# Reordering the first units of a decoder-layer kernel: scores, transposed scores, maxima rows and input fetches

## The reference

```
x = layernorm(x + attn(x))            # 16 heads of 16, causal within a window of 64
x = layernorm(x + xattn(x, ctx))      # relu on q, k, v; causal; + q; its own layernorm
x = layernorm(x + ffn(x))             # 8 experts, top 2, two groups, capacity 160 each
```

## Time and profile before

| | us |
|---|---|
| median of 3 runs | 633.37 (625.5 to 636.76) |
| the profiled execution | 631.15 |
| its span | 629.4 |
| PE busy in the span | 524.6 (83%) |
| DVE, ACT, POOL busy | 337.2, 218.4, 147.0 |

### The profile page before, as it was taken

The page is one execution under the profiler, slowest core; times in us unless marked ns, Lnnn a source line. Parts: engine busy times, 40 slices in busy tenths (PEclk is TensorE's granted clock), DMA queues, the critical chain, the costliest instruction groups (busy, mean ns, idle before and its releaser), DMA issues. The chain is left out here.

```text
span 629.4 us, 12845 instructions
## 1 busy us (share of the span) xinstructions
PE 524.6 (83%) x5092; PEld 405.5 (64%) x5092; DVE 337.2 (54%) x952; ACT 218.4 (35%) x491; POOL 147.0 (23%) x160
## 2 busy tenths in 40 slices
PE   5067749889889999999999889699898999999960
PEld 4044527666667676666677656477677888888850
DVE  3436524665767877877768967774364112242114
ACT  2001223534435445544545525352521011222103
POOL 5010002101102102102223257000213755231330
PEclk9667788989989999999999989799999999999995
DMA  3999473492492591592556565455667634898214
GB/s 116 202 190 170 142 187 46 62 118 45 65 119 37 82 141 29 78 138 34 78 79 93 76 114 167 64 185 185 198 224 254 202 53 74 234 291 266 22 16 140
DMA packets 56760, 78.97 MB, mean 125 GB/s; under 512 B 9294, under 2 KB 49357, under 8 KB 53628
## 3 DMA queue, kind: packets, MB, share of 16 engines
q1 hardware_dynamic: 42524, 39.64, 38.5%
q10 hardware_dynamic: 8032, 33.21, 16.8%
q0 software_dynamic: 6144, 5.29, 5.2%
HBM read 40.32 MB, written 13.74 MB: 86 GB/s over the span
## 5 line engine op out<-in xcount | busy, mean ns | idle before, releaser
L938 DVE TENSOR_REDUCE negm<-nat 128x4 f32<-128x512 f32 (+2 forms) x192 | 120.1, 641 | 98.9 <-PE nat L521 97.1
L755 ACT ACTIVATE probs<-byk 128x512 f32<-128x512 f32 (+1 forms) x192 | 105.9, 563 | 114.0 <-PE byk L521 112.3
L521 PE MATMUL nat<-arena 96*128 96x128 bf16 (+2 forms) x512 | 73.8, 248 | 0.0
L521 PE MATMUL byk<-arena 99*128 99x128 bf16 (+2 forms) x512 | 71.6, 242 | 0.0
L1192 POOL TENSOR_TENSOR resk<-fk,parts_k 128x512 f32<-128x512 f32 x8 | 9.3, 1158 | 229.2 <-ACT fk L697 194.6
L517 PE MATMUL nat<-window_q,identb 128*128 128x384 bf16 (+1 forms) x96 | 36.0, 375 | 28.3 <-DMA arena<-parts_k 21.5
L521 PEld LDWEIGHTS nat<-arena 96*128 96x128 bf16 x512 | 47.0, 102 | 16.9 <-issue 3.5
L521 PEld LDWEIGHTS byk<-arena 99*128 99x128 bf16 x512 | 45.6, 99 | 17.4 <-issue 0.9
L517 PE MATMUL byk<-window_k,identb 128*128 128x384 bf16 (+1 forms) x96 | 34.0, 354 | 15.1 <-DMA arena<-mT 14.5
L659 PE MATMUL work<-yn_T,arena 128*128 128x160 f32 x256 | 40.1, 305 | 2.4 <-DVE r_s L1103 2.4
L659 PE MATMUL work<-woT,arena 128*128 128x160 f32 x256 | 39.8, 304 | 0.0
(11 more groups left out here) (189 smaller groups left out, 917.2 us busy)
## 6 DMA issues: line engine op xcount, KB each, us to landing
arena<-parts_q SPq DMA_DIRECT2D x96, 128.0 KB, 5.1
arena<-parts_k SPq DMA_DIRECT2D x96, 128.0 KB, 5.4
arena<-in_ffn_wi ACTq DMA_DIRECT2D x12, 1024.0 KB, 5.1
arena<-in_ffn_wo ACTq DMA_DIRECT2D x12, 1024.0 KB, 8.3
expert_x<-fq ACTq DMA_DIRECT2D x1, 2600.0 KB, 12.6
v_s<-expert_x SPq DMA_DIRECT2D x20, 130.0 KB
xres<-in_x ACTq DMA_DIRECT2D x1, 2048.0 KB, 28.1
token_y<-xres SPq DMA_DIRECT2D x8, 256.0 KB, 4.7
```

What stands on the lines that cost most here:

```text
L521: last = nc.tensor.matmul(bank[:, i * w:(i + 1) * w], lhsT, rhs, start=False, stop=(i == heads - 1), skip_group_check=True)
L755: nc.scalar.activation(dst, src, ACT.Exp, scale=0.25).then_inc(exp_ready, 1)
L938: V.tensor_reduce(dst, src, AX, ALU.max, negate=True).then_inc(nat_free[job % 2], 1)
```

## The change

- Unit 0's twelve N jobs run without a break. QS2, KS2 and VS0 move behind them and behind MP0 and MT0; T0.0 follows before N1.0. In PE's order: N0.0 to N0.11, MT0, QS2, KS2, VS0, T0.0, N1.0, T0.1, N1.1, and so on; QS3 comes after N1.5.
- T, PV, YA, YB, Y2, WO, R3 and L3 come sooner by 6.05, 4 and 2 slots in units 0, 1 and 2 (`SOONER`), MT at 11.5, 12.6 and 13.2 instead of 14. In unit 1 PE's order becomes N1.11, N2.0, MT1, N2.1, PV0.3, T1.0.
- In units 0 to 2 ACT issues the three DMAs of the maxima rows itself, right after its copy to mT, and SP doesn't.
- `LOADS` has new slots. x_T of batch 2, the value weights and `rows` go out only when unit 0's k stack has landed (a wait on ACT); x_T of batch 3 after KS2; woT, the cross attention's weights, the contexts and the router's weights at slots 16 to 50.
- xres is fetched batch by batch (XL, 256 KB each) at 8 slots into an s unit (14 in unit 0), each with a semaphore of its own.
- The clear of expert_x becomes four DMAs of 650 KB, in the s units of batches 4 to 7, from a pattern in `ranked`, with runs of 1040 bytes where there were 4160. The wait for it moves from ACT's QC to DVE's GA, before `ranked` is first written; POOL's GS keeps its own.
- The memset of the cross attention's value tile moves behind SK1 on DVE.

```diff
-LOADS = ((-20, 0), (-17.3, 1), (-16, 2), (-5, 3), (-4, 4), (2, 5), (6, 6), (14, 7), (22, 8), (26, 9))
+LOADS = ((-20, "x1"), (-16, "one_s"), (-4, "one_c"), (-3, "x2"), (-2.9, "wv"), (-2.8, "rows"), (11.84, "x3"), (16, "wo"), (20.5, "ck"), (21, "c0"),
+         (26, "cq"), (40, "c1"), (41, "cv"), (50, "wr"))
+CLEARS = (4, 5, 6, 7)
+SOONER = {0: 6.05, 1: 4, 2: 2}
+ROWS_BY_ACT = 3
...
-    return first_slot(k) + 18 + j
+    return first_slot(k) + 18 - SOONER.get(k, 0) + j
...
-                    add(n0 + 9.6, "LX", UNIT_OF["s", later])
+                    add(n0 + (14.6 if b == 0 else 9.6), "LX", UNIT_OF["s", later])
...
+            add(n0 + (14 if b == 0 else 8), "XL", k)
+            for at, name in ((-12.4, "QS"), (-12.35, "SQ"), (-12.3, "KS"), (-12.2, "SK")) if b == 2 else ((-19, "QS"), (-18, "SQ"), (-17.5, "KS"), (-16.5, "SK")):
+                add(n0 + at, name, k)
+            for at, name in ((11.85 if b == 0 else 8.5, "VS"), (20, "XB"), (34 - sooner, "Y2"), (35 - sooner, "WO"), (36 - sooner, "R3"), (36.8 - sooner, "L3")):
...
-        add(n0 + 12, "MP", k)
-        add(n0 + 14 if k < last else 195.6, "MT", k)
+        add(n0 + (11.3 if k == 0 else 12), "MP", k)
+        add(n0 + {0: 11.5, 1: 12.6, 2: 13.2}.get(k, 14) if k < last else 195.6, "MT", k)
...
             def MT(k, n, layer, b):
+                if k < ROWS_BY_ACT:
+                    return
                 emptied(sp, "MT", k)
...
                 nc.scalar.activation(mT[:, k % 2, :], bank[0:MR * H, :].bitcast(BF16)[:, 0:T], ACT.Copy).then_inc(released("MT", k), 1)
+                if k < ROWS_BY_ACT:
+                    emptied(act, "MT", k)
+                    for i in range(MR):
+                        nc.scalar.dma_start(stack["q", k % PAIRS][KR + i:KR + i + 1, :, :], mT[i * H:(i + 1) * H, k % 2, :])\
+                            .then_inc(m_rows[k % 2], 16)
...
+                if what in ("x1", "x2", "x3"):
+                    to = int(what[1])
+                    if to == 2:
+                        act.wait_ge(stacked["k"][0], SIDE)
+                    nc.scalar.dma_start(x_T(to), a["x_T"][to]).then_inc(x_in[to], 16)
...
+            def XL(k, n, layer, b):
+                nc.scalar.dma_start(xres[:, b * QT:(b + 1) * QT, 0:D], x_v[:, b * QT:(b + 1) * QT, :]).then_inc(xres_in[b], 16)
...
-                if b == 0:
-                    act.wait_ge(zeros_ready, 1)
-                    nc.scalar.dma_start(x_dram.rearrange("(p n a) d -> p n (a d)", p=P, a=4),
-                                        no_rows.unsqueeze(1).broadcast_to([P, E * GROUPS * CAP // P // 4, 4 * ROW])).then_inc(cleared, 16)
+                if b in CLEARS:
+                    part = E * GROUPS * CAP // P // len(CLEARS)
+                    at = CLEARS.index(b) * part
+                    if at == 0:
+                        act.wait_ge(zeros_ready, 1)
+                    nc.scalar.dma_start(x_dram.rearrange("(p n) d -> p n d", p=P)[:, at:at + part, :],
+                                        no_rows.unsqueeze(1).broadcast_to([P, part, ROW])).then_inc(cleared, 16)
```

More of the change, by code:

```diff
@@ L93, in in_order @@
         n0 = first_slot(k)
+        sooner = SOONER.get(k, 0)
         if layer == "s":
@@ L96, in in_order @@
                 if earlier == b:
-                    add(n0 + 9.6, "LX", UNIT_OF["s", later])
+                    add(n0 + (14.6 if b == 0 else 9.6), "LX", UNIT_OF["s", later])
             if b == 3:
                 add(n0 + 9.7, "LC", UNIT_OF["c", 2])
-            for at, name in ((-19, "QS"), (-18, "SQ"), (-17.5, "KS"), (-16.5, "SK"), (8.5, "VS"), (20, "XB"),
-                             (34, "Y2"), (35, "WO"), (36, "R3"), (36.8, "L3")):
+            add(n0 + (14 if b == 0 else 8), "XL", k)
+            for at, name in ((-12.4, "QS"), (-12.35, "SQ"), (-12.3, "KS"), (-12.2, "SK")) if b == 2 else ((-19, "QS"), (-18, "SQ"), (-17.5, "KS"), (-16.5, "SK")):
+                add(n0 + at, name, k)
+            for at, name in ((11.85 if b == 0 else 8.5, "VS"), (20, "XB"), (34 - sooner, "Y2"), (35 - sooner, "WO"), (36 - sooner, "R3"), (36.8 - sooner, "L3")):
                 add(n0 + at, name, k)
@@ L114, in in_order @@
             add(t_slot(k, j), "T", k, j)
-        add(n0 + 12, "MP", k)
-        add(n0 + 14 if k < last else 195.6, "MT", k)
+        add(n0 + (11.3 if k == 0 else 12), "MP", k)
+        add(n0 + {0: 11.5, 1: 12.6, 2: 13.2}.get(k, 14) if k < last else 195.6, "MT", k)
         for g in range(G):
[L118 to L121, removed]
+            add(n0 + 22.2 - sooner + 3 * g if k < last - 1 else t_slot(k, 3 * g + 2) + (1.1 if g < G - 1 else 0.5), "PV", k, g)
+        add(n0 + 32.6 - sooner if k < last - 1 else (198.6, 206.9)[k - last + 1], "YA", k)
+        add(n0 + 32.9 - sooner if k < last - 1 else (198.7, 207.0)[k - last + 1], "YB", k)
+    for i, (at, _) in enumerate(LOADS):
         add(at, "LD", i)
@@ L278, in flat @@
             return tile[tuple([slice(None)] * len(tile.shape))].rearrange(f"p {names} -> p ({names})")
-        no_rows = flat(fq, "s c t")[:, X1S * C * T - 4 * ROW:]
+        no_rows = flat(ranked, "a t e")[:, 0:ROW]
         wi, wo = [], []
@@ L300, in attention_and_experts @@
         ws_in = sem("ws_in"); bias_in = sem("bias_in"); w_s_v_in = sem("w_s_v_in"); rows_in = sem("rows_in"); w_s_o_in = sem("w_s_o_in")
-        wc_in = {n: sem(f"w_c_{n}_in") for n in "qkv"}; wr_in = sem("wr_in"); xres_in = sem("xres_in")
+        wc_in = {n: sem(f"w_c_{n}_in") for n in "qkv"}; wr_in = sem("wr_in"); xres_in = sems("xres_in", B)
         x_in = sems("x_in", TOK + 1); c_in = sems("c_in", TOK)
@@ L716, in QC @@
                     computed(act, "FQ", UNIT_OF["c", b - X1S])
-                elif b == 1:
-                    act.wait_ge(cleared, 16)
                 parts_free("q", k)
@@ L787, in LD @@
             def LD(i, n, layer, b):
[L789 to L792, removed]
+                what = LOADS[i][1]
+                if what in ("x1", "x2", "x3"):
[3 more added lines that the diff above has]
+                    nc.scalar.dma_start(x_T(to), a["x_T"][to]).then_inc(x_in[to], 16)
+                elif what in ("c0", "c1"):
+                    to = int(what[1])
+                    nc.scalar.dma_start(cT[:, to, :, :], a["ctx_T"][to]).then_inc(c_in[to], 16)
+                elif what in ("cq", "ck", "cv"):
+                    nc.scalar.dma_start(wc[what[1]][:, :, :], a["w_" + "_".join(what)]).then_inc(wc_in[what[1]], 16)
+                elif what == "wv":
@@ L793, in LD @@
                     nc.scalar.dma_start(ws[:, :, 2 * D:3 * D], a["w_s_v"]).then_inc(w_s_v_in, 16)
-                elif i == 2:
+                elif what == "rows":
                     nc.scalar.dma_start(rows[:, :, :], a["rows"].partition_broadcast(P)).then_inc(rows_in, 16)
[L796 to L799, removed]
+                elif what == "wo":
@@ L800, in LD @@
                     nc.scalar.dma_start(woT[:, :, :], a["w_s_o"]).then_inc(w_s_o_in, 16)
[L801 to L810, removed]
+                elif what == "wr":
@@ L811, in LD @@
                     nc.scalar.dma_start(wr[:, :, :], a["w_router"]).then_inc(wr_in, 16)
+            x_v = a["x"].rearrange("b (t p) d -> p (b t) d", p=P)
+            def XL(k, n, layer, b):
+                nc.scalar.dma_start(xres[:, b * QT:(b + 1) * QT, 0:D], x_v[:, b * QT:(b + 1) * QT, :]).then_inc(xres_in[b], 16)
             def WL(i, n, layer, b):
@@ L858, in _ @@
             walk({"QS": QS, "KS": KS, "KC": KC, "QC": QC, "XC": copy_out("XC", x1_T), "Y2": copy_out("Y2", yn_T, "WO"),
-                  "XR": copy_out("XR", x2_T, "RT"), "MT": MT, "T": T_, "PV": PV, "R1": R1, "R2": R2, "R3": R3, "GC": GC, "XB": clear, "LD": LD, "WL": WL,
+                  "XR": copy_out("XR", x2_T, "RT"), "MT": MT, "T": T_, "PV": PV, "R1": R1, "R2": R2, "R3": R3, "GC": GC, "XB": clear, "XL": XL, "LD": LD, "WL": WL,
                   "XT": XT, "H0": hidden("H0", range(0, 3)), "H2": hidden("H2", range(6, 8)), "FR": FR, "FN": FN})
@@ L898, in LD @@
             def LD(i, n, layer, b):
-                if i in (2, 3):
-                    link(V.memset(vone["sc"[i - 2]][:, :, :, :, :], 1.0))
+                if LOADS[i][1] in ("one_s", "one_c"):
+                    link(V.memset(vone[LOADS[i][1][4]][:, :, :, :, :], 1.0))
             def SC(k, n, layer, b):
@@ L1042, in GA @@
                 emptied(dve, "RT", UNIT_OF["c", (n + 1) * GB - 1])
+                if n == 0:
+                    dve.wait_ge(cleared, 16 * len(CLEARS))
                 tiles = slice(n * GT, (n + 1) * GT)
@@ L1196, in XB @@
             def XB(k, n, layer, b):
-                if b == 0:
-                    pool.wait_ge(xres_in, 16)
+                pool.wait_ge(xres_in[b], 16)
                 if b == 0:
@@ L1224, in GS @@
                         pool.wait_ge(numbered, 1)
-                        pool.wait_ge(cleared, 16)
+                        pool.wait_ge(cleared, 16 * len(CLEARS))
                     put_gates(tile, GT, 0)
```

## The result

The kernel after the change takes 625.12 us (median; 622.7 to 632.02), the kernel before beside it 633.05: a ratio of 0.9894, with a 95% interval of 0.9877 to 0.9912. It is 1.1% faster, where 611 us, 3.2% under the profiled execution before, were forecast, and 625 lies above the range. The profiled execution took 624.59 us (span 622.8), 6.6 us under the one before.

The account below looks back on a forecast made before the run. It took a start waiting for DMA, then a long run bound by PE. Lead to T0.0 17.9, plus T1.0 3.3, less T2.0 1, made 20.2 us: 631.15 to 611 us, forecast 603 to 618 (chance 0.75), range 600 to 623.

Parts of the forecast that it names:

- Step 1: Unit 0's k stack lands earlier without bulk loads: N0.0 at 26.0 instead of 36.3 us, gain 10.3 (0 to 12.8).
- Step 2: From N0.0 to T0.0: T0.0 at 45.1 us (43 to 47) instead of 66.58; lead including unit 0's stack 17.9.
- Step 3: PE's waits at MT1 and T1.0 for unit 1's maxima: 5.8 us instead of 9.1, gain 3.3 (0.3 to 4.7).
- Step 4: T2.0 charged 1 us (0 to 5.4); clear and residual in parts, moved memset and moved waits cost 0.
- The postponed loads collide one stage later: At QS3, N2.0 and T1.0: transfers land as in the crowded start, 10.5 us more, 621.5 us; chance 0.14.
- The stack copies set their own pace: At N0.0: 12 copies land no sooner without bulk loads, N0.0 near 36, 10.3 us lost, 621 us; chance 0.07.
- ScalarE is held: Among T0's and T1's exps: issuing six 256 KB loads holds ACT, at 8.97 us each 665 us; chance 0.04.

## Why the prediction was wrong

The direction held: faster, the gain won in the start and carried to the end whole, and no sign of the long run being bound by anything but PE. The size, 20.2 us, did not hold. Step by step:

**Step 1, unit 0's stack.** Forecast 26.0, measured 28.5 us. The step took the landing of six copies with the queue otherwise empty. Here twelve follow each other at 118 GB/s: by that rate 12 x 128 KB from 14.0 us on are done at 27.3 (an estimate). A loss of 2.5 us. The mechanism was right: with the old fetching N0.0 is at 36.8.

**Step 2, T0.0.** Forecast 45.1, measured 49.4: the 2.5 above and 1.8 more. MT0 came nearly as worked out (11.35 us behind N0.0 for 11.0); x_T 2 cost 1.1 us, as it had to wait for unit 1's copies; and QS2 and KS2 ran at the low clock, where the middle of both had been taken (granted 0.53 from 40 to 44 us):

```profile
41.27 6.56 PE L478 MATMUL work<-xT,ws 128*128 128x256 f32 x16 [1.13 <-DMA xT<-in_x_T]
```

QS3 found its input, so the 1.5 us charged there were not spent.

**Step 3, T1.0: the step that failed.** I took a landing of 3.3 us for unit 1's rows, "nearer to the quiet landing, because ACT's and SP's large transfers are spaced out by then". They were not: unit 3's twelve copies end their issue in the very moment in which the rows start theirs, and the rows land when these copies are through, 9 us after the last issue. PE's two waits were 11.7 us (1.2 at MT1) instead of 5.8: 5.9 us lost. Holding the copies back leaves 2.6 us at T1.0, so they are what the step left out. My upper bound, 6.3 us, was no bound: it was the median landing of one busy stretch of the old order, not worked out from the copies that would stand ahead in the new one. The old trace already went beyond it: T0.0 at 66.58 came 7.5 us after the issue of its rows ended at 59.1, and unit 2's copies had been issued just ahead of these rows, too:

```profile
52.05 3.84 SPq L390 DMA_DIRECT2D arena<-parts_k  x6
```

And part of what PE wins before T1.0 becomes a longer wait there: with the early loads MT1 came 3.8 us sooner than after the change (64.8 us instead of 68.6) and T1.0 only 2.3.

**Step 4, the rest.** T2.0 was charged 1 us; it cost 2.2 and another 1.3 at QC of the first cross unit. For that the timelines of ScalarE and PE have the reason:

```profile
101.13 2.00 ACTq L754 DMA_DIRECT2D arena<-mT  x3
103.17 0.60 ACT L744 ACTIVATE x_T<-work 128x512 f32<-128x512 f32 x1 [2.08 <-issue]
...
103.87 1.97 PE L478 MATMUL work<-x_T,wq_c 128*128 128x256 f32 x8 [1.33 <-issue]
```

Sending three rows takes ScalarE 2.0 us, and the copy of the transposed x1, which QC needs, stands behind it. T3.0's 4.9 us I had not seen at all. Unit 3's own slots are unchanged, but `SOONER` took two T jobs of unit 2 from in front of T3.0, and SyncE still sends these rows behind unit 5's copies. Which of the two counts for how much no run tells; with those copies held and ScalarE sending, all waits for rows up to 150 us are 3.0 us.

The misses are 2.5 + 1.8 - 1.5 + 5.9 + 2.5 (T2.0 and QC, 3.5 for 1) + 4.9 = 16.1 us, which leaves 4.1 of the 20.2; 6.6 were measured. Of the other 2.5 us, 1.9 may be a wait of PE on DVE's split of k (4.2 us in two pieces before, 2.3 in one after), but other short waits changed as well, so this is not shown; the rest is unassigned.

**The rivals.** "The postponed loads collide one stage later" had the place (T1.0) and the wrong cause: x_T 3, the loads and unit 2's stack were in time, and taking loads away changed nothing. "The stack copies set their own pace" was nearest to the truth, but I asked it only of N0.0, not of every later transfer behind copies. "ScalarE is held" cost PE the 1.3 us at QC here and no more that its waits show, and is real in the run with the early clear. The Trainium skill's rule ("DMA: Bandwidth & Descriptors", "Rules for kernel authors") that another issuing engine brings no bandwidth agrees with these runs: with loads in ScalarE's queue beside SyncE's copies the rate stayed at 119 GB/s from 28 to 38 us. The same rule says that DMAs of several issuing engines interleave; here, behind copies, they did not: in the run with the loads on SyncE no packet of ScalarE's queue moved from 71 to 76 us. What the sender saved at T1.0, 5.1 us, is in part its place behind SyncE's other issues: there the rows' issue starts 2.6 us later and takes 1.5 longer; the rest no run explains.

## What to carry to other kernels

When a small transfer decides, look at which large ones are issued just ahead of it on any queue, and price it by their end, not by its own quiet landing. Part of what is won by bringing its consumer forward is then lost in a longer wait; holding the large transfers back until it has landed costs one semaphore wait, if their own consumer has slack (here unit 3's copies could go 11 us later without a wait at N3.0). And a bound for an unseen landing must be worked out for the new neighbours, not taken from the worst row of the old order.

## What the runs showed of the hardware that was not expected

- Stack copies (128 KB each, on-chip to on-chip) fill the DMA engines at 118 GB/s; when few copies were left, loads ran with them at 251 GB/s from 40 to 44 us.
- Loads and rows issued on ScalarE's queue behind such copies on SyncE's landed only when these were through (12.8 us for 256 KB, some 9 for 8 KB). What puts the second queue off is not shown. Yet 768 KB of loads issued among the copies, moved behind the rows or away, left T1.0 between 80.4 and 81.8 us, while the residual's 2048 KB and the other early loads, issued ahead of unit 0's k copies, moved N0.0 by 8 us. Why the small amount is free and the large one isn't stays open.
- A load issued behind the four clears held ScalarE's own instructions for 9.62 us.
